# Last layer norm and feed-forward part joined in one stage, with the output stored tile by tile

## What is computed

```python
def _ghost_linear(x, idx, lut):
    w = lut[idx]
    return jnp.einsum('bsh,oh->bso', x, w)
gate = _ghost_linear(x, gate_idx, lut)
up = _ghost_linear(x, up_idx, lut)
h = jax.nn.silu(gate) * up
return _ghost_linear(h, down_idx, lut)
...
x = x + _L1_ffn_ref(_layernorm(x, axis=-1), L1_ffn_lut, L1_ffn_gate_idx, L1_ffn_up_idx, L1_ffn_down_idx)
return x
```

## Time and profile before

| | us |
|---|---|
| Median of 3 runs | 2719.22 (2717.35 to 2721.97) |
| The profiled execution's own time | 2724.37 |
| Its span, first to last instruction | 2722.9 |
| TensorE busy in the span | 2405.8 (88%) |
| VectorE busy | 1578.6 (58%) |
| ScalarE busy | 964.8 (35%) |
| GpSimd busy | 973.7 (36%) |

### The profile page before, as it was taken

How to read it: one execution, slowest core, us unless ns; L and a number is a source line. 1 busy time by engine, 2 the same in 40 slices (tenths; PEclk the granted TensorE clock), 3 DMA queues, 4 the chain that set the end, 5 groups by cost and what they waited for, 6 DMA issues and landing times. The chain is left out here.

```text
span 2722.9 us, 48580 instructions
## 1 busy us (share of the span) xinstructions
PE 2405.8 (88%) x12839; PEld 1823.4 (67%) x12840; DVE 1578.6 (58%) x3443; ACT 964.8 (35%) x2184; POOL 973.7 (36%) x878
## 2 busy tenths in 40 slices
PE   7969999994756999999999759999979898899996
PEld 5845555552635888888888638888855454688885
DVE  6235556662665445555555466999178786555553
ACT  3114555542144334444444322222255453222211
POOL 3138888883202556666666301111111111000000
PEclk9978999996865999999999979999989999799998
DMA  5469999994344899999998544547498640100001
GB/s 171 125 175 322 342 343 343 336 337 112 86 178 138 233 259 257 256 246 270 263 249 212 83 145 138 174 159 224 135 250 184 163 116 12 36 23 23 23 9 62
DMA packets 263261, 491.18 MB, mean 180 GB/s; under 512 B 31841, under 2 KB 149089, under 8 KB 253410
## 3 DMA queue, kind: packets, MB, share of 16 engines
q1 hardware_dynamic: 197154, 272.17, 33.5%
q0 software_dynamic: 62976, 212.42, 27.4%
q10 hardware_dynamic: 3024, 5.29, 0.6%
HBM read 592.96 MB, written 198.79 MB: 291 GB/s over the span
## 5 line engine op out<-in xcount | busy, mean ns | idle before, releaser
L1378 PE MATMUL m_ps_u<-m_ring,m_xT_hi 128*128 x1280 | 374.3, 354 | 34.9 <-DMA m_ring<-w_split 34.7
L1344 POOL DMA_INDIRECT expert_sum<-x_res,token_of x160 | 253.1, 1582 | 231.7 <-ACT x_res L1446 141.5
L1378 PEld LDWEIGHTS m_ps_u<-m_ring,m_xT_hi 128*128 128x128 f32 x1280 | 239.4, 192 | 39.0 <-issue 38.5
L790 ACT ACTIVATE probs<-ps_c 128x512 f32<-128x512 f32 (+3 forms) x384 | 182.8, 490 | 225.1 <-PE ps_c L723 138.4
L820 DVE TENSOR_REDUCE neg_max<-ps_r 128x1 f32<-128x512 f32 (+3 forms) x256 | 147.6, 589 | 168.5 <-PE ps_r L690 116.6
L1378 PE MATMUL m_ps_u<-m_ring,m_xT_lo 128*128 x640 | 218.9, 342 | 0.0
L1501 DVE SCALAR_TENSOR_TENSOR m_h<-m_silu,m_xg,m_ps_u 128x128 f32<-128x128 f32 x160 | 55.6, 348 | 276.7 <-ACT m_silu L1440 276.7
L1337 POOL DMA_INDIRECT m_xg<-x_rows,token_of x160 | 175.9, 1099 | 103.5 <-issue 98.7
L690 PE MATMUL ps_r<-k_st,q_st 96*128 96x512 f32 (+3 forms) x384 | 164.0, 434 | 49.8 <-DVEq L813 21.6
L1814 PE MATMUL s_ps<-s_x_lo,s_w_hi 128*128 128x512 f32 x512 | 201.5, 394 | 0.0
L1814 PE MATMUL s_ps<-s_x_hi,s_w_lo 128*128 128x512 f32 x512 | 200.2, 391 | 0.0
(11 more groups left out here) (337 smaller groups left out, 5804.5 us busy)
## 6 DMA issues: line engine op xcount, KB each, us to landing
m_ring<-w_split SPq DMA_DIRECT2D x160, 1536.0 KB
m_ring<-w_split SPq DMA_DIRECT2D x160, 768.0 KB
w_split<-e_gu_parts POOLq DMA_DIRECT2D x32, 1536.0 KB
proj<-s_out SPq DMA_DIRECT2D x32, 1024.0 KB, 4.1
e_raw_gu<-w_experts POOLq DMA_DIRECT2D x32, 768.0 KB
w_split<-e_dn_parts POOLq DMA_DIRECT2D x32, 768.0 KB
e_raw_dn<-w_experts POOLq DMA_DIRECT2D x32, 512.0 KB
q_st<-q_parts SPq DMA_DIRECT2D x32, 256.0 KB, 6.3
```

The source lines that it names most:

```text
L790: nc.scalar.activation(probs[a][j % RING][:, :width], ps_c[a][:, :width], ACT.Exp, scale=SCALE).then_inc(exp_done, 1)
L1344: pool.indirect_dma_start(acc[j % 2], rows_at(j), y[j % TURNS], None, bounds_check=PADDED - 1, oob_is_err=True, compute_op=ALU.add).then_i ...
L1378: last = nc.tensor.matmul(ps_u[b % 2][:, :W_UP], x[b % 2][:, k, :], ring[:, first + k * GU_ROW:][:, bass.ds(place, W_UP)], start=(n == 0), ...
```

## The change

`store_tokens` and the call of `layernorm_transposed` go; `lut_feed_forward` gets their work in its own block.

- TensorE turns the four tiles of group 0, then makes the gate and up products of runs 0, 1 and 2 (`first_up`, `AHEAD = 3`), and within each, between gate and up product, turns the four tiles of the next group. It turns into the four `ps_o` tiles, which the down products use later. Then come the down products of runs 0 and 1, one after the other, the up product of run 3, the down product of run 2, and the old order from there.
- VectorE computes the moments of group 0, normalizes its four tiles and makes their low parts, and takes the moments of the second group after that; `xn` has four buffers. Per group it then has four normalizations, the moments of the group after the next, four low parts, and the hidden product and its low part of the run.
- ScalarE has the square roots of the later groups between the silus.
- SyncE loads the first weight tile into a buffer of its own (`f_first`) and goes on to the next weight tiles without a wait; at the end it issues one store per token tile when the last sum of the tile is there.
- GpSimd splits the first weight tile as before.
- The first body of eight runs is written out and no longer part of the loop.

The pieces of the diff stand in the order SyncE, GpSimd, TensorE, ScalarE, VectorE; the helpers of ScalarE and VectorE that hold one step of the norm each (`deviations`, `high_x`, `moments`, `scales`, `normalize`, `low_x`, `hidden`, `low_h`) hold the instructions of L156 to L203 and L2450 to L2492 for one group, tile or run.

```diff
-def store_tokens(nc, x_res, out):
-    with ExitStack() as ctx:
-        stored = ctx.enter_context(nc.semaphore("out_stored"))
-        block = ctx.enter_context(nc.Block())
-
-        @block.sync
-        def _(sp):
-            sp.dma_start(out.rearrange("(n p) d -> p n d", p=P), x_res[:, :, :]).then_inc(stored, 16)
-            sp.wait_ge(stored, 16)
...
-        first = [(m[:, :, :P], by_k(w_hi[0][:, part, :]), by_k(w_lo[0][:, part, :])) for part, m in ((0, gate), (1, up))]
-        first.append((down[:P, :], w_hi[0][:, 2, :], w_lo[0][:, 2, :]))
-        layernorm_transposed(nc, "f_ln", x_res, x_hi, x_lo, ident, first)
+        first = sb("f_first", [P, PARTS, 512])
...
+        AHEAD = 3
+        tiles_of = lambda g: range(g * SUB, (g + 1) * SUB)
+        turned = [t[:, :].rearrange("p (k t) -> p k t", k=KD) for t in ps_o]
...
+            for part, w in ((0, gate), (1, up)):
+                sp.dma_start(by_k(first[:, part, :]), w[:, :, :P]).then_inc(first_loaded, 16)
+            sp.dma_start(first[:, 2, :], down[:P, :]).then_inc(first_loaded, 16)
...
+            out_rows = out.rearrange("(n p) d -> p n d", p=P)
+            for i in range(TILES):
+                sp.wait_ge(added, SUB + BODIES * RUNS * SUB + i + 1)
+                sp.dma_start(out_rows[:, i, :], x_res[:, i, :]).then_inc(stored, 16)
+            sp.wait_ge(stored, 16 * TILES)
+
+        @block.gpsimd
+        def _(pool):
+            for part in range(PARTS):
+                pool.wait_ge(first_hi_done, part + 1)
+                nc.gpsimd.tensor_tensor(w_lo[0][:, part, :], first[:, part, :], w_hi[0][:, part, :].bitcast(F32), ALU.subtract).then_inc(first_lo_done, 1)
 
...
+            def turn(i):
+                pe.wait_ge(xn_ready, i + 1)
+                if i >= SUB:
+                    pe.wait_ge(x_lo_done, i - SUB + 1)
+                for k in range(KD):
+                    last = nc.tensor.transpose(turned[i % SUB][:, k, :], xn[:, i % SUB, k * P:(k + 1) * P], ident[:, :])
+                last.then_inc(transposed, 1)
+
+            def first_up(r):
+                pe.wait_ge(x_lo_done, (r + 1) * SUB)
+                pe.wait_ge(h_done, r + 1)
+                for ps, part in ((ps_g, 0), (ps_u, 1)):
+                    if r == 0:
+                        pe.wait_ge(first_lo_done, part + 1)
+                    terms = [(w_hi[0], x_hi), (w_lo[0], x_hi), (w_hi[0], x_lo)]
+                    for m, (k, (w, x)) in enumerate([(k, t) for k in range(KD) for t in terms]):
+                        last = nc.tensor.matmul(ps[r % 2][:, :], w[:, part, k * P:(k + 1) * P], x[:, k, r * GROUP:(r + 1) * GROUP],
+                                                start=(m == 0), stop=(m == 3 * KD - 1))
+                    if part == 0:
+                        for i in tiles_of(r + 1):
+                            turn(i)
+                last.then_inc(up_done, 1)
 
...
+                if isinstance(n, int) and n == 0:
+                    pe.wait_ge(x_lo_done, TILES)
+                    pe.wait_ge(first_lo_done, PARTS)
...
-            up_product(0, 0)
-            with pe.Fori(0, BODIES - 1) as it:
+            for i in tiles_of(0):
+                turn(i)
+            for r in range(AHEAD):
+                first_up(r)
+            body(0, False, AHEAD)
+            with pe.Fori(1, BODIES - 1) as it:
                 body(it, False)
...
             act.sem_inc(w_hi_done, PARTS)
-            with act.Fori(0, BODIES - 1) as it:
+            deviations(0)
+            act.wait_ge(first_loaded, 16 * PARTS)
+            for part in range(PARTS):
+                nc.scalar.copy(w_hi[0][:, part, :], first[:, part, :]).then_inc(first_hi_done, 1)
+            for i in tiles_of(0):
+                high_x(i)
+            for r in range(AHEAD):
+                deviations(r + 1)
+                for i in tiles_of(r + 1):
+                    high_x(i)
+                silu_of(0, r)
+                if r < 2:
+                    high_h(0, r)
+            for r in range(RUNS):
+                if r >= AHEAD:
+                    silu_of(0, r)
+                if r >= 2:
+                    high_h(0, r)
+                if r % GROUPS < PARTS:
+                    split_next(split_hi, 0, r)
+            with act.Fori(1, BODIES - 1) as it:
                 body(it, False)
...
+            moments(0)
+            scales(0)
+            for i in tiles_of(0):
+                normalize(i)
+            for i in tiles_of(0):
+                low_x(i)
+            moments(1)
+            for r in range(AHEAD):
+                scales(r + 1)
+                for i in tiles_of(r + 1):
+                    normalize(i)
+                if r + 2 < GROUPS:
+                    moments(r + 2)
+                for i in tiles_of(r + 1):
+                    low_x(i)
+                hidden(0, r)
+                if r < 2:
+                    low_h(0, r)
+            for r in range(RUNS):
+                if r > 0:
+                    add_run(0, r - 1)
+                if r >= AHEAD:
+                    hidden(0, r)
+                if r >= 2:
+                    low_h(0, r)
+                if r % GROUPS < PARTS:
+                    split_next(split_lo, 0, r)
+            add_run(0, RUNS - 1)
+            with dve.Fori(1, BODIES - 1) as it:
                 body(it, False)
```

More of the change, by code:

```diff
@@ L2335, in _, with lut_feed_forward @@
                 add_out(BODIES - 1, 1, tt)
-def lut_feed_forward(nc, x_res, ident, w_ffn):
+def lut_feed_forward(nc, x_res, ident, w_ffn, out):
     RUNS = 2 * GROUPS
@@ L2396, in up_product @@
                     pe.wait_ge(w_lo_done, it * 2 + r // GROUPS + 3)
+                if isinstance(n, int) and n == AHEAD:
+                    pe.wait_ge(x_lo_done, TILES)
                 pe.wait_ge(h_done, n + 1)
@@ L2414, in down_product, with body @@
                 last.then_inc(down_done, 1)
-            def body(it, final):
+            def body(it, final, begun=1):
                 runs = runs_of(final)
                 for r in range(runs):
-                    if r + 1 < runs:
+                    if r + 1 < begun:
+                        pass
+                    elif r + 1 < runs:
                         up_product(it, r + 1)
@@ L2443, in split_hi, with silu_of, high_h @@
                 nc.scalar.copy(w_hi[b][:rows, part, :], raw[b][:rows, part, :]).then_inc(w_hi_done, 1)
+            def silu_of(it, r):
+                rows = rows_of(it)
+                act.wait_ge(up_done, it * RUNS + r + 1)
+                nc.scalar.activation(silu[r % 2][:rows, :], ps_g[r % 2][:rows, :], ACT.Silu).then_inc(silu_done, 1)
+            def high_h(it, r):
+                n, rows = it * RUNS + r, rows_of(it)
+                act.wait_ge(h_done, n + 3)
+                act.wait_ge(down_done, n + 1)
+                nc.scalar.copy(h_hi[r % 2][:rows, :], h[r % 2][:rows, :]).then_inc(hi_done, 1)
@@ L2445, in body @@
             def body(it, final):
-                rows = rows_of(it)
                 for r in range(runs_of(final)):
-                    n, r2 = it * RUNS + r, r % 2
-                    act.wait_ge(up_done, n + 1)
-                    nc.scalar.activation(silu[r2][:rows, :], ps_g[r2][:rows, :], ACT.Silu).then_inc(silu_done, 1)
-                    act.wait_ge(h_done, n + 3)
-                    act.wait_ge(down_done, n + 1)
-                    nc.scalar.copy(h_hi[r2][:rows, :], h[r2][:rows, :]).then_inc(hi_done, 1)
+                    silu_of(it, r)
@@ L2454, in body, with deviations, high_x @@
+                    high_h(it, r)
                     if r % GROUPS < PARTS and not final:
                         split_next(split_hi, it, r)
-            act.sem_inc(w_hi_done, PARTS)
-            with act.Fori(0, BODIES - 1) as it:
+            def deviations(q):
+                act.wait_ge(var_done, q + 1)
+                nc.scalar.activation(std[:, group_of(q)], var_eps[:, group_of(q)], ACT.Sqrt).then_inc(std_done, 1)
+            def high_x(i):
+                act.wait_ge(transposed, i + 1)
+                nc.scalar.copy(x_hi[:, :, toks_of(i)], turned[i % SUB][:, :, :]).then_inc(x_hi_done, 1)
@@ L2495, in body, with moments, scales, normalize @@
                 add_run(it, runs - 1)
-            with dve.Fori(0, BODIES - 1) as it:
+            def moments(q):
+                for i in tiles_of(q):
+                    nc.vector.bn_stats(stats[:, i, :], x_res[:, i, :]).then_inc(stats_done, 1)
+                dve.wait_ge(stats_done, (q + 1) * SUB)
+                for i in tiles_of(q):
+                    nc.vector.bn_aggr(mv[:, i, :], stats[:, i, :]).then_inc(aggregated, 1)
+                dve.wait_ge(aggregated, (q + 1) * SUB)
+                nc.vector.tensor_scalar_add(var_eps[:, group_of(q)], mv[:, group_of(q), 1], LN_EPS).then_inc(var_done, 1)
+            def scales(q):
+                dve.wait_ge(std_done, q + 1)
+                nc.vector.reciprocal(rstd[:, group_of(q)], std[:, group_of(q)]).then_inc(rstd_done, 1)
```

(10 more changed lines are left out.)

28 lines of the change are left out of this document (20 added, 8 removed).

## The result

The changed kernel takes 2689.5 us (median of 4 runs, 2682.74 to 2694.55) and the kernel before 2720.59 (4 runs, 2717.35 to 2723.07): ratio 0.9888, 95% interval 0.9865 to 0.9911. In a later series it was 2682.76 (5 runs) against 2719.52 (9 runs), 0.9867 (0.9843 to 0.9890). The forecast was 2692.1 in a range of 2686 to 2702.

What follows compares the result with a forecast made beforehand. TensorE was taken to bound the kernel, idle in the norm's stage and during the final store; 17.2 us from the start plus 9.9 from the store, 27.1 off the median 2719.22, gave 2692.1, range 2686 to 2702.

Steps and rivals of the forecast that it cites:

- First product at 9.9: Start of the norm's stage: first product begins 9.9 us after the stage begins, before at 37.67, so 27.8 us sooner.
- First set 5.2, full clock from there: First twelve matmuls of the new start: 5.2 us at half clock, the other seven sets at full clock in 19.0.
- Turns 5.6: Transposes of the twelve later tiles, now among the first products: 5.6 us of TensorE time in all.
- Waits 0.8, 0.9, 2.3, 0.7, 0.9, together 5.6: TensorE's five waits among the first products, reckoned mostly from VectorE's order of work: 5.6 us in all.
- Fourth group's product at 45.3: End of the new start: fourth group's first product 45.3 us after the stage begins instead of 62.5, 17.2 us saved.
- Table loads at 1.28 and nothing else: ScalarE's switches between square root and silu: six loads instead of two, each 1.28 us with nothing added behind it.
- Store, 3.5 from the last addition to the end: Program's end: sixteen stores of 256 KB, the last landing in 3.0 us, some 3.5 to the end; 9.9 us saved.
- half clock throughout: Rival, 9%: waits keep TensorE at half clock through the whole beginning, only 7.4 us gained, 2712 us.
- a clock that doesn't come back: Rival, 2%: interleaved turns and waits keep TensorE's clock low, 2.4 us per further set of twelve; 2741 with 12 sets.
- an order that changes nothing: Rival, 3%: parts meant to overlap in the start wait for each other, only the store gains; 2709 us.
- the table's: Rival, 6%: each ScalarE table switch costs a drain of 1.28 us beyond its load, some 3.2 in all; 2695.3 us.
- the store that isn't hidden: Rival, 6%: small stores pass the queue slower than one large one; 7.8 us saved instead of 9.9, at worst nothing, 2702.

Runs made afterwards that it cites:

- more-tables run: Changed kernel with one unused exponential ahead of the third and the fourth square root, so two further table loads on the path; 2688.96 us in one run.
- norm-apart run: Kernel before with only the output changed, sixteen stores of one token tile in place of the single one; 2704.79 us, ratio 0.9969.

## Why the prediction was right

- **First product at 9.9:** 9.50. The weight casts, said to be hidden by the turns, were not: the loads landed late enough for them to run from 4.75 to 6.4 and the high parts waited. But the four low parts then ran back to back (2.53), so the end came out the same.
- **First set 5.2, full clock from there:** 4.49; eight matmuls at half clock, four at full. The seven others kept the pace of 2.72 for twelve from one matmul to the next, and took 2.81 to 3.01 each with what comes at their edges (see the waits). By the more-tables run the time saved in the first set is worth nothing: at 2.85 instead of 4.49 the second gate product came no sooner.
- **Turns 5.6:** 1.67, 1.78 and 1.79, together 5.2. The forecast's own figures (1.04, three of 0.36, eight of 0.46) add up to 5.8 and not to the 5.6 that it took.
- **Waits 0.8, 0.9, 2.3, 0.7, 0.9, together 5.6:** 1.65, 0.55, 1.98, 0.55, 0.88, together 5.6; the order of work after a wait adds 1.5 more (the first matmul behind each takes 0.50 in place of 0.39, and the last one before it drains). The first was twice the forecast, for a reason worth seeing: TensorE was through its first pair 1.3 us sooner than reckoned, while VectorE's low parts came when they were due (last one done at 20.2, 20.7 reckoned). Where the other engine sets the pace, time saved on TensorE turns into waiting.
- **Fourth group's product at 45.3:** 45.36. The sum is better than its terms, and that is luck: 0.4, 0.7 and 0.4 too much in product, clock and turns against 1.5 too little behind the waits.
- **Table loads at 1.28 and nothing else:** shown, here and with two more of them.
- **Store, 3.5 from the last addition to the end:** 2.74, as the pieces land in 2.2 and not in 3.0. The term was 10.65 instead of 9.9, shown by the norm-apart run.
- **Nothing in the long stretch:** 335.17 against 335.03. The first body, now written out and no loop any more, cost or gave nothing there.
- **Median 2692.1:** 2689.5 and 2682.76, which is 31.1 and 36.8 under the kernel before where 27.1 was forecast. The last part accounts for 27.7 of either. The second median lies 3 us below the stated range, so that the first came within 2.6 us of the forecast is partly luck: the scatter ahead of the last part (over 18 us in six traces) is larger than the 2 us that the range allowed for the spread of the runs. The mechanism is borne out by the lengths of the last part, not by the medians.

Of the rivals, half clock throughout, a clock that doesn't come back and an order that changes nothing fall with the timeline of the start; the table's falls with the two loads 1.50 apart; the store that isn't hidden falls with the norm-apart run. Among the products of the new start the clock fell only behind waits that experiments made longer or put close together.

## What to carry to other kernels

When a per-tile preparation stage stands ahead of a matmul-bound one, count how little of it the first product needs, put the rest between products, and then price the gain by the engine that prepares, not by TensorE: here its order of work set the new start, and each wait removed uncovered the next in line (moments, then square roots behind silu). Output whose parts are final before the end can be stored in parts; only the last part's landing then stays. Compare profiles from a common instruction at the start of the changed part, since what lies ahead may scatter by more than the change brings.

## What was not expected of the hardware

- TensorE kept the full clock behind waits of 1.65 and 1.98 us, but ran at half clock behind 4.18 and 5.98, and also behind 1.97 and 2.06 with twelve matmuls between; behind 0.40 and 2.47, again with twelve between, it kept the full clock. In the program's own end it was at half clock behind 4.54.
- Of the first set of twelve, eight matmuls were at half clock in the first trace of the changed kernel and all twelve at full clock in the more-tables run, behind the same instructions.
- Two function table loads 1.50 us apart with a function of 0.20 between them.
- Stores of 256 KB landed in 2.2 us (median of 16), while one of 4096 KB took 12.8.
